# Three fixed orders of steps worked out anew in an attention and expert kernel

## The reference, cut to what matters

```
xn = layernorm(x)
qkv = xn @ w_qkv + b_qkv              # 16 heads of 8: 4 causal over all rows, 12 causal in a window of 32
s = softmax(q k / sqrt(8)) v @ w_out + b_out
score = sigmoid(xn @ gate_w.T)        # 16 experts in 4 groups; the best 2 groups, in them the best 4 experts
y = sum over chosen experts of weight * down(silu(gate(xn)) * up(xn)) + a shared expert
out = x + s * silu(xn + y)
```

## Time and profile before

| | |
|---|---|
| median of 3 runs | 579.53 us (579.01 to 580.9) |
| the profiled execution, its own time | 581.03 us |
| its span | 579.2 us |
| mean granted TensorE clock | 0.965 |
| PE, busy | 516.5 us (89%) |
| DVE, busy | 429.8 us (74%) |
| ACT, busy | 332.7 us (57%) |
| POOL, busy | 179.6 us (31%) |
| chain that ended last | PE 48%, DVE 32%, issue 7%, ACT 6% |
| first `qfull` of the four batches, the ends of opening and bodies | 67.1, 199.7, 332.35, 465.02 us |

### The profile page before, as it was taken

The page is one execution under the profiler, slowest core; times in us unless marked ns, Lnnn a source line. Parts: engine busy times, 40 slices in busy tenths (PEclk is TensorE's granted clock), DMA queues, the critical chain, the costliest instruction groups (busy, mean ns, idle before and its releaser), DMA issues.

```text
span 579.2 us, 10586 instructions
## 1 busy us (share of the span) xinstructions
PE 516.5 (89%) x3930; PEld 301.7 (52%) x3960; DVE 429.8 (74%) x937; ACT 332.7 (57%) x646; POOL 179.6 (31%) x167
## 2 busy tenths in 40 slices
PE   1768999899998999899998999999998999989992
PEld 1636665555445665555445655545454755644440
DVE  6786697786698788886789788786779776877423
ACT  3544556656855457555865367564875457455851
POOL 3413431033524441024423442023342632003311
PEclk9957999998999999998999999998999999999996
DMA  9200000000000300000000300000000110000001
GB/s 233 73 1 0 2 1 1 2 1 2 0 1 2 110 2 2 1 1 1 1 2 1 94 16 3 1 1 1 1 2 0 37 38 1 3 1 0 1 1 36
DMA packets 17933, 9.82 MB, mean 17 GB/s; under 512 B 2502, under 2 KB 17754, under 8 KB 17882
## 3 DMA queue, kind: packets, MB, share of 16 engines
q1 hardware_dynamic: 17552, 8.85, 5.6%
q10 hardware_dynamic: 330, 0.30, 0.3%
HBM read 7.05 MB, written 2.10 MB: 16 GB/s over the span
## 4 chain that ended last, share of the span: by engine, by line
PE 48%; DVE 32%; issue 7%; ACT 6%; DVEq 3%; POOL 2%; DMA 1%; POOLq 0%; ACTq 0%
PE bank L746 6%; DVE kpad L1061 4%; DVE mxp L1146 4%; PE bank L629 4%; DVE mxp L1144 4%; PE bank L513 4%; PE bank L515 4%; PE bank L514 4%; PE bank L690 3%; DVE qpad L1048 3%; PE bank L659 3%; PE bank L706 3%; DVE denT L1085 3%; PE bank L730 2%; DVE hid L1100 2%
## 5 line engine op out<-in xcount | busy, mean ns | idle before, releaser
L889 ACT ACTIVATE stage<-bank 128x512 f32<-128x512 f32 (+3 forms) x240 | 112.7, 521 | 62.8 <-PE bank L663 41.7
L1220 POOL TENSOR_TENSOR hid<-hid,wrow 128x512 f32<-128x512 f32 x64 | 82.2, 1286 | 171.6 <-DVE hid L916 171.6
L1144 DVE TENSOR_REDUCE mxp<-bank 128x1 f32<-128x512 f32 (+4 forms) x192 | 89.8, 517 | 14.0 <-PE bank L632 8.2
L1100 DVE SCALAR_TENSOR_TENSOR hid<-hid,bank 128x512 f32<-128x512 f32 x72 | 48.9, 680 | 54.7 <-ACT hid L809 54.5
L746 PE MATMUL bank<-hid,down_w 128*128 128x512 f32 x144 | 76.0, 609 | 0.0
L1211 POOL TENSOR_TENSOR maxd<-mxp,k 128x512 f16<-128x512 f32 x32 | 36.4, 1137 | 117.9 <-DVE mxp L1146 64.0
L809 ACT ACTIVATE hid<-bank 128x512 f32<-128x512 f32 x72 | 43.3, 601 | 48.2 <-PE bank L515 47.4
L513 PE MATMUL bank<-xh,up_hi 128*128 128x512 f32 x144 | 60.8, 422 | 2.4 <-DVE hid L916 1.8
L514 PE MATMUL bank<-xh,up_lo 128*128 128x512 f32 x144 | 57.8, 401 | 0.0
L515 PE MATMUL bank<-xl,up_hi 128*128 128x512 f32 x144 | 57.4, 399 | 0.0
L659 PE MATMUL bank<-kpad,kall 128*128 128x512 f16 (+3 forms) x192 | 54.8, 329 | 2.1 <-ACT stage L889 1.7
(11 more groups left out here) (162 smaller groups left out, 1002.4 us busy)
## 6 DMA issues: line engine op xcount, KB each, us to landing
xin<-in_L_attn_x_dram SPq DMA_DIRECT2D x4, 512.0 KB, 4.2
xres<-in_L_attn_x_dram SPq DMA_DIRECT2D x4, 512.0 KB, 4.1
out_dram<-xres SPq DMA_DIRECT2D x8, 256.0 KB, 2.3
k<-in_c_dram SPq DMA_DIRECT2D x1, 576.0 KB, 5.8
stage<-in_L_ffn_Wg_dram SPq DMA_DIRECT2D x1, 512.0 KB, 6.0
stage<-in_L_ffn_Wu_dram SPq DMA_DIRECT2D x1, 512.0 KB, 5.9
stage<-in_L_ffn_Wd_dram SPq DMA_DIRECT2D x1, 512.0 KB, 7.4
k<-in_c_dram ACTq DMA_DIRECT2D x1, 216.5 KB, 3.9
```

What stands on the lines that cost most here:

```text
L889: act.activation(prob[:, t % NPROB, 0:cols], ps[:, 0:cols], ACT.Exp).then_inc(freed, 1)
L1100: dve.scalar_tensor_tensor(out=hid[:, i % NHID, :], in0=hid[:, i % NHID, :], scalar=1.0, in1=banks[at.bank(gate)][:], op0=ALU.add, op1=ALU ...
L1144: ins = dve.tensor_reduce(mxp[:, c, j:j + 1], ps[:, 0:cols], AX_X, ALU.max)
L1220: pool.tensor_tensor(hid[:, i % NHID, :], hid[:, i % NHID, :], wrow[:, iw % NWT, :], ALU.mult)\
```

## The change

The three order strings are replaced. Each new string has the same letters the same number of times, so no step is added, dropped or altered; only the weave is new, and with it which bank a product gets. In words, what the prediction speaks of:

- Opening: `fill 0, setup, small, stats, fill 1, ln` instead of `stats, fill 0, ln, setup, small, fill 1`; the first weight tile ahead of `xT`, two more ahead of `gate`; `vn.0` ahead of `k.1`; `kpads.0` and two `max` steps behind the last routing part instead of before it.
- Body: `ctx.0.0` from behind `times.1.6` to before `times.1.4` and the routing; `times.1.5` ahead of `route.3`; `ctx.0.1` ahead of `pads.0`; `route.6` ahead of the last maxima of group 0; `times.0.0`, `times.0.1` and `maxdone.0.1` ahead of `mul.0`.
- Last section: the last four `down` steps behind the last `pv`, with `fold.1` between the first and the second of them; `up.1.7` and `up.1.8` later among the scores; `ctx.1.0` and `ctx.1.1` ahead of `z.1`.

```
--- before.py
+++ after.py
@@ -144,14 +144,14 @@
     return out
 
 
-FIRST_ORDER = ("PIPPIIIPPPIITPPITPIPTITIPPTPIPPTIPPPPPTIPPIITTVXXVXVXXVXVXVXXXVVXXVXVXX")
-BODY_ORDER = ("AAPAARXAAXAXRRARRAAARAAAAXXRPAAARAAXAXAARRAXRRAAAARRRAXAARAAPXARAAAAAAAXAAARXAAARAXAAAAXXRRRARAR"
-              "RAAARAAAAARRARRAAARRRARAXARAAXAXRRRRARAPRAARXRRRRAAAARRRXAXRAXRRRAXRRARARAARPRRPARAXRRXXRTRXRRRR"
-              "RTPRTRRRRPRRTXRRRRRRXXXRXRCRPRPRRRXXXRPPRPRRRRRPRRRTPCRRXXRPRRRRRTRRXPRXPRXRPPRRRRRXRRRTXXRRRRRT"
-              "TRPCXPC00XVXXVXXVVVX01XXXX1X1VXVVVVXX")
-LAST_ORDER = ("AAAAAAAXAARAARAAAXXRARXRAAAAARRARAAAXAXRRRAXARXAXARAARAAARRARAAAAAAAAAXAARAXAAAXXARAXRRRARRARAAA"
-              "RAAAARARAAXRARRXRRRXRRRAAAAAAAARAAAARAAARAXRAXRRAXAAXRRRRAARRXRRRXRRRRRRRRAAXRRRXRXCXRRRRXCRRRRR"
-              "RRRRRRXXRRRRRRRXRRRRXRRXRRRRXXRRRRXRRRRR0RXXRRRRRRRXRRRRRRXRRRRRRRXXR0XCC0111")
+FIRST_ORDER = ("IIIPIPPIPPIIPTPPTPTTIIVPIPPPIIPTPTIPPITPPPPITTVXPVXVXXVXXVXXXXVVVXXVXXX")
+BODY_ORDER = ("PAAAAXAAXARRXRARAARAAARXAAPXXAARAARAAXAARRXAARRAARAPRXRAAAAARXAARAAAAAAAXAAAXRAARAXAAAXXARRRRAAA"
+              "RRRRAAAAAAARARRAAARRRARRAXAAAXXRRRARRAARXRRRRAAARRXRRAAPAAXRARXRRARRARRAAAPRRRXPAARXRRRXRPCRRRXT"
+              "RRXTRRRRTXXRTRRRRRPRRRRRXRXXPRPRRXXRRPRRPRXRRRPCPRRPRTTRRXRRRRRRTRRRXXPRRPXXPRRRPPXRRRRRXXRRRRRT"
+              "TRPCXCX0VXXPVX0X11VX0XXXV1XXVVXVVVVXX")
+LAST_ORDER = ("AAAAAAAXAARXAXRRAARAXAARAAAAAARRRRAAARAXRXAARXXRXAARAAAAARRARAAAAAAAAXAARAXAAAXXAAXRRARRRARRAAAA"
+              "RAAAARARAAXRARXRRRRXRRRAAAAARAAARAXAAXRRXARAXRRRRAAAAAARAARARXRRRRXRRRRRRAARXRRXXRRXRRCRRRXRRRXC"
+              "RRRRRRRXRRXRRXRRRRRRRRRRRRRRRRRRRRXRRRXRRRR0RRRRRRRXRXRRRRRRRXRRX0XCCXXXX0111")
 
 
 FIRST_EXPERTS = expert_steps(0) + [("z", 0), ("z2", 0)]
```

## The result

The changed kernel took 565.24 us (median of 4 runs, 564.81 to 567.38) beside 580.21 for the kernel before (579.01 to 582.41): a ratio of 0.9745, 95% interval 0.9705 to 0.9785. It is 15.0 us faster. The forecast was 5.5 us, with 574.0 as the time and 569.5 as the low end: the direction is right, the size is wrong by a factor of nearly three.

What follows compares the result with a forecast made beforehand. PE was taken to bound the bodies, a chain through other engines the opening, a tail where PE mostly stands the last section's end. Opening -0.9, bodies -1.8, last section -2.8 sum to -5.5: 574.0 us, its own range 571.5 to 576.5.

Steps and rivals of the forecast that it cites:

- The wait of 1.03 goes to about 0.2: -0.8: Body: times.1.5 ahead of route.3 shortens PE's wait for pair 5, -0.8 us a body; ends -1.03 and +1.75.
- Front half: Body's front halves: neighbouring steps (times.0.8 and ln.1, up.0.7 and qfull) exchange places, neither engine gains work: 0.
- Late part: Body after ctx.0.1 moves ahead of pads and last routing parts: DVE almost gapless, trades places, 0; ends -1.0 and +1.0.
- +0.2 for mul.0: Body: POOL's mul.0, behind two expert products and maxdone, ends later and delays PE's outT: +0.2 us, ends 0 and +1.5.
- Opening, -0.9: Opening: cw ready as before, vn.0 no longer ahead of the experts, half its gain taken: -0.9 us, ends -1.9 and +3.6.
- the 1.9 for vn.0: Opening: after cw, PE has no vn.0 (1.91 us) left to do ahead of the experts: -1.9.
- Last section, -2.8: Last section: later down products -2.6, ACT +0.7, earlier fold copy -0.4, clock -0.5: -2.8 us; ends -1.0 and -4.5.
- the +0.7 for ACT: Last section, scores 28 to 38: no expert step there, so ACT's exponentials outlast PE's work: +0.7 us charged.
- Rival A: Opening: the late normalisation passes through, +3.6 instead of -0.9 us; kernel 578.5, no difference; chance 0.12.
- B: Rival, bodies: DVE enters its gapless stretch 1.0 us earlier, each body -1.6; kernel 571.0 us; chance 0.15.
- C: Rival, bodies: DVE's routing slowed beside POOL's work, three bodies cost +6.6 us; kernel slower, 582.5; chance 0.12.
- D: Rival, last section: three down products bring little as ACT bounds the last scores, -1.0; kernel 575.8 us; chance 0.11.

Runs made afterwards that it cites:

- e13: Kernel before with one body move, down.1.2 and times.1.5 from behind five scores to directly ahead of route.3: 572.65 us beside 580.66, ratio 0.9856.
- e5: Kernel before with only body steps 0 to 181 (up to the first half's fourth expert pair) in the new order: median 575.84 us, ratio 0.9915.
- e6: Kernel before with only body steps 225 to 324 (ctx.0.1 ahead of pads, to the body's tail) in the new order: ratio 0.9946.
- e14: Changed kernel with times.1.5 moved one routing part back, behind route.3: 581.54 us, ratio to the kernel before 1.0002.
- e1: Kernel before with only the opening's order new: 580.21 us against 580.71, ratio 1.0003.
- e3: Kernel before with only the last section's order new: 576.96 us against 580.71, ratio 0.9933.
- e8: Kernel before with only the tail of the last section new, scores and expert steps before it in the old order: ratio 0.9948.

## Why the prediction missed, step by step

- **The failed step: "The wait of 1.03 goes to about 0.2: -0.8"**, with the ends -1.03 and +1.75. The mechanism was right and the sign too; the size of the term is what failed. That one move measured -2.8 us a body by the kernel's time (e13, 8.4 us for three bodies) and -2.3 by its one profile, not -0.8. Its stages show how: a body with the fall gives 1.4 (132.7 to 131.3), one without it 2.5 (132.4 to 129.9). I read one wait from one execution and took it as the most that its removal can bring. It was the smaller of two values, 1.03 and 2.29, and it also swallowed whatever time the rest of the body gained.
- The remainder of the size is in how many bodies have the fall. With a wait of 1 us or more for times.1.5, 15 of 22 profiled bodies had it; with none or less, 11 of 29. The executions without a profile point the same way: the median granted clock was 0.976 over e13's five and 0.967 over the 17 of before beside them. Why is open: the fall comes 15 us ahead of the wait, and e5 had the wait and none of the falls. The forecast had no term for it.
- Front half, "0": measured -0.5 to -0.6. Ahead of gate the second body of before has six waits of PE of over 0.3 us, 2.8 in all, four of them for row maxima; the changed one has three, 1.3 in all. That the shorter waits make the 0.5 to 0.6 is argued.
- Late part, "0": from gate to fold.1, beyond the wait, -0.3, and -0.2 from there to the end of the body. Alone it was worth 3.1 (e6); the two sum to 1.5 over three bodies, and where the rest comes from no run shows.
- "+0.2 for mul.0": 0. It ended at 315.13, outT came at 315.25 without a wait.
- Opening, -0.9: -1.6, and that it came near is in part luck. The walk to cw nearly held: ready 0.2 later in this profile (forecast within 0.1) and 0.4 later in the mean, because its last operation takes 0.5 more beside POOL. The profile's -2.8 overstates: over all kernels with the old opening and its full work the mean is 66.1 (8 profiles), with the new one 64.5 (7). But nothing of it is vn.0's at the place where I counted it: the first weight product starts at 49.4 in the mean of the old ones (47.5 to 50.4) and at 49.5 in that of the new (48.5 to 50.4). Both of my terms ahead of it, the 1.9 for vn.0 and what stands against it, cancelled. The gain lies behind it, where I had none: 16.7 us to the first `qfull` in every old opening, 15.0 to 15.2 in every new one. There v.0.0, 0.9 us of products, is already done, and PE waits 0.03 instead of 0.78.
- Last section, -2.8: -3.6. The last attention product ends 2.3 us earlier (forecast -1.9: the +0.7 for ACT was somewhat too much; PE is busy 29.57 of 30.12 us, 0.55 short). Behind it 1.3 are gone (forecast 0.9): the last projection ran at the higher level, 0.95 less where I charged 0.5.
- Rival A: no. B: right that bodies gain more and short in the size (1.6 against 2.4 in the mean); its reason, DVE earlier in its gapless stretch, no run tests by itself. C: its collisions did come, and their price (`g` 1.15 for 0.19), and PE doesn't pay because times.1.5 stands ahead of route.3; e14 is rival C, at +5 a body against the changed kernel. D: no.

Whole sum: opening -1.6 to -2.8, bodies -7.3, last section -3.6, against -0.9, -1.8, -2.8.

## What to carry to other kernels

A wait read in one execution isn't the upper bound of what its removal brings: look at it in every body of every profile at hand, for it absorbs what other stretches gain and grows when they do. Where a queue in order puts a product's operand behind a chain of small operations, ask first what stands directly ahead of it; one such move measured as much here as the whole new list of the body. Before pricing a chain on DVE at its lone durations, see which of its operations fall beside POOL, and what happens when they shift by a microsecond.

## What the runs showed of the chip that I had not expected

A two-input DVE operation of the routing, 0.19 to 0.29 us alone, takes up to 1.1 to 1.4 us when it starts just behind a POOL product of 1.16 to 1.29: over all profiles such operations ended 0.05 to 0.16 us behind POOL's, whatever their own size (32 or 128 columns). It isn't only two-input operations: the small select `gm` (0.18 alone) took 0.62 to 0.98 beside POOL, and an f16 copy of 0.28 (L1068) up to 1.31. And not every operation is held: `hid` from a PSUM bank (0.68, L916) started 190 times within a POOL instruction and was never stretched, nor were the maxima (MAX8, 0.16) in 322.

A PE rest of 2.3 to 3.4 us amid dense work was followed by the lower clock in all three bodies of e14, in e1 (2.54) and in e6 (2.30), and one of 2.29 in e3 and e8 was not. The fall behind gate comes and goes between bodies of one execution with the same instructions, and costs 1.2 to 1.4 us of a body that isn't waiting elsewhere (changed kernel, e13).
